# A two-layer decoder on one core: other orders on four engines, the values of the mixture split before the clearings, and another order at the feed-forward's end

## The reference, cut to what matters

```
x = x + L0_attn(layernorm(x))               # 16 query heads of 32, one key and one value head
x = x + L0_xattn(layernorm(x), ctx)         # a mix of features
x = x + L0_ffn(layernorm(x), 4-bit weights) # 1408 hidden: down(silu(gate) * up), then y / rms(y)
x = x + L1_attn(layernorm(x))               # 16 heads, then an out-projection with a bias
x = x + L1_xattn(layernorm(x), ctx, mask)   # 16 query heads of 128, 8 key and value heads, then Wo
x = x + L1_ffn(layernorm(x))                # a mixture: 32 experts of rank 16, the best 2 of each row

def ffn(x):
    gate, up = split(x @ dequant(gate_up).T)
    y = (silu(gate) * up) @ dequant(down).T
    return y / sqrt(mean(y * y) + eps)
```

## Time and profile before

| | us |
|---|---|
| median of 3 runs (2445.82 to 2447.76) | 2447.39 |
| profiled execution | 2444.98 |
| its span | 2443.2 |
| TensorE busy | 2354.3 |
| VectorE busy | 1730.4 |
| ScalarE busy | 1197.0 |
| GpSimd busy | 159.5 |

### The profile page before, as it was taken

One profiled execution on the slowest core, in us unless ns is written; L12 is line 12 of the kernel. 1 busy time (PEld: TensorE's weight loads), 2 busy tenths in 40 slices (PEclk: granted clock), 3 DMA queues, 4 the chain that ended last, 5 costly groups with the idle time before them and its releaser, 6 DMA issues. The chain is left out here.

```text
span 2443.2 us, 37409 instructions
## 1 busy us (share of the span) xinstructions
PE 2354.3 (96%) x11266; PEld 1740.2 (71%) x11266; DVE 1730.4 (71%) x3717; ACT 1197.0 (49%) x2346; POOL 159.5 (7%) x281
## 2 busy tenths in 40 slices
PE   7899999999999899999989999999999999999798
PEld 5555557777777688555557777777777777777677
DVE  6578888877877654667656766667776767667863
ACT  3467766533233522567745544444444444444641
POOL 0000000000000000000031000001010101010200
PEclk9999999999999999999999999999999999999999
DMA  5722201000000235443302000000000000001001
GB/s 169 201 75 72 69 20 69 1 1 0 0 0 1 77 118 181 121 101 93 77 31 74 1 13 12 9 13 9 13 14 8 17 4 17 4 9 45 1 18 52
DMA packets 71922, 110.51 MB, mean 45 GB/s; under 512 B 14266, under 2 KB 25274, under 8 KB 71194
## 3 DMA queue, kind: packets, MB, share of 16 engines
q1 hardware_dynamic: 71834, 109.38, 15.0%
HBM read 75.26 MB, written 34.08 MB: 45 GB/s over the span
## 5 line engine op out<-in xcount | busy, mean ns | idle before, releaser
L3446 DVE SCALAR_TENSOR_TENSOR x_res<-xa_out_bank,xa_den,x_res 128x512 f32 (+1 forms) x256 | 191.6, 748 | 139.2 <-PE xa_out_bank L2921 138.6
L3295 ACT ACTIVATE xa_pT_hi<-xa_t_bank 128x512 fp32r<-128x512 f32 x256 | 149.6, 597 | 128.1 <-PE xa_t_bank L3117 128.1
L333 DVE TENSOR_REDUCE l1s_mx<-l1s_max_bank 128x1 f32<-128x512 f32 x256 | 156.5, 682 | 68.7 <-PE l1s_max_bank L188 68.6
L3306 ACT ACTIVATE xa_prob<-xa_prob,xa_nmax 128x512 f32<-128x512 f32 x256 | 182.7, 715 | 29.6 <-DVE xa_nmax L3413 29.6
L3395 DVE TENSOR_TENSOR xa_pT_lo<-xa_t_bank,xa_pT_hi 128x512 fp32r<-128x512 f32 x256 | 175.7, 687 | 24.1 <-ACT xa_pT_hi L3295 23.8
L333 DVE TENSOR_REDUCE l0s_mx<-l0s_max_bank 128x1 f32<-128x512 f32 x256 | 156.9, 683 | 46.8 <-PE l0s_max_bank L188 46.7
L3413 DVE CUSTOM_DVE_ANT_0 xa_prob<-xa_s_bank,xa_mask_bias 128x512 f32<-128x512 f32 x256 | 171.1, 687 | 22.6 <-PE xa_s_bank L2921 10.9
L3099 PE MATMUL xa_bank_a<-xa_xT_hi,xa_q_w 128*128 (+1 forms) x512 | 180.1, 393 | 0.0
L2921 PE MATMUL xa_out_bank<-xa_o_w,xa_o_hi 128*128 128x512 f32 x512 | 170.2, 413 | 9.5 <-DVE x_res L3446 8.4
L2123 DVE SCALAR_TENSOR_TENSOR ffn_yT<-ffn_y,ffn_ysc,ffn_yT 128x512 f32<-128x512 f32 x164 | 120.6, 746 | 42.5 <-PE ffn_y L1849 42.4
L3117 PE MATMUL xa_t_bank<-ident,xa_prob 128*128 128x128 f32 x1024 | 149.9, 274 | 0.0
(11 more groups left out here) (506 smaller groups left out, 5673.9 us busy)
## 6 DMA issues: line engine op xcount, KB each, us to landing
l0s_q<-l_q SPq DMA_DIRECT2D x96, 128.0 KB, 2.4
l1s_q<-l_q SPq DMA_DIRECT2D x96, 128.0 KB, 3.1
l1s_k<-l_k SPq DMA_DIRECT2D x96, 128.0 KB, 3.2
l0s_k<-l_k SPq DMA_DIRECT2D x96, 64.0 KB, 2.5
x_res<-in_x_dram SPq DMA_DIRECT2D x4, 1024.0 KB, 9.4
l_q<-l_q_hi SPq DMA_DIRECT2D x16, 256.0 KB, 2.5
l_q<-l_q_lo SPq DMA_DIRECT2D x16, 256.0 KB, 3.2
l_q<-l_hi SPq DMA_DIRECT2D x16, 256.0 KB, 2.1
```

The source lines that it names most:

```text
L333: dve.tensor_reduce(self.mx[:, j // QT, j % QT:j % QT + 1], self.max_bank[j % 3][:], AX.X, ALU.max)\
L3295: act.activation(pT_hi[:, kt % (QT - 1), :], t_bank[kt % 2][:], ACT.Copy).then_inc(pT_hi_done, 1)
L3306: act.activation(prob[:, q, :], prob[:, q, :], ACT.Exp, bias=nmax[:, q:q + 1], scale=-1.0, accum_out=den[:, r, 0, q:q + 1]).then_inc(exp_d ...
L3446: dve.scalar_tensor_tensor(xt, out_bank[:], den[:, r, 2, q:q + 1], xt, ALU.mult, ALU.add)\
```

## The change

It has seven parts.

1. Start. The first load of x is cut into two halves with a semaphore each, and VectorE takes the statistics of tiles 0 and 1 behind the first one. The three bias loads get a semaphore of their own, which ScalarE waits for before its first `take`; TensorE waits for the three weight loads alone.
2. Behind layer 1's attention TensorE gets four more matmuls, whose result nobody reads.
3. Feed-forward, TensorE: down product 0 stands behind 10 gate passes, not 8; product 1 behind all 12 and 2 up passes; product 2 behind 7 up passes, not 6.
4. Feed-forward, ScalarE: the nine scalings stand behind `silu(c, 1)`, not ahead of it; in the last chunk `take_h` stands ahead of a `keep`.
5. Feed-forward's end, VectorE: the additions of y stand ahead of the statistics, and the last one ahead of `combine`.
6. Out-projection. GpSimd adds 12 biases, waits for the first scales, adds the last four and waits twice more between the pieces of weights. TensorE projects the first queries ahead of product 15; ScalarE and VectorE take them early. VectorE takes the first maximum ahead of the last `combine`, and it now normalises tiles 12 to 15, which was ScalarE's.
7. Mixture. The tiles are dealt out anew, so that GpSimd splits the values first and then waits for the turned weights and clears `mix_gT_hi`.

```diff
@@ -711,15 +712,18 @@
-            load_x(0)
+            half = S // 2
+            for n, loaded in enumerate((x_loaded[0], x_half_loaded)):
+                sp.dma_start(st.x[:, n * QT // 2:(n + 1) * QT // 2, :],
+                             x_in[0, n * half:(n + 1) * half].rearrange("(q p) d -> p q d", p=P)).then_inc(loaded, 16)
...
             sp.dma_start(bias[:, 0:KC], Wq_b.rearrange("(f p) -> p f", p=P), allow_slow_non_contiguous=True)\
-                .then_inc(w_loaded, 16)
+                .then_inc(bias_loaded, 16)
...
                 sp.dma_start(bias[n * HD:(n + 1) * HD, KC:NF], column(w), allow_slow_non_contiguous=True)\
-                    .then_inc(w_loaded, 16)
+                    .then_inc(bias_loaded, 16)
@@ -804,7 +808,7 @@
             pe.wait_ge(made, 2)
-            pe.wait_ge(w_loaded, 16 * 6)
+            pe.wait_ge(w_loaded, 16 * 3)
@@ -851,6 +855,8 @@
             def take(b, f):
+                if b == 0 and f == 0:
+                    act.wait_ge(bias_loaded, 16 * 3)
@@ -918,7 +924,11 @@
                 dve.wait_ge(x_loaded[b], 16)
-                norm.stats(dve, b, batch_tiles(b))
+                for t in range(b * QT, (b + 1) * QT):
+                    if t == QT // 2:
+                        dve.wait_ge(x_half_loaded, 16)
+                    norm.tile_stats(dve, t)
+                norm.combine(dve, b, batch_tiles(b))
@@ -1642,6 +1652,8 @@
         att.tensor(pe, turn_out_weights)
+        for _ in range(4):
+            pe.matmul(att.max_bank[2][:], self.st.ident_r[:], self.ow[0][:, 0, :], start=True, stop=True)
@@ -1892,21 +1904,22 @@
                         turn_next(0)
-                        gate_up(c, s, b, 0, 4, 8)
+                        gate_up(c, s, b, 0, 4, 10)
...
                         finished(0)
-                        gate_up(c, s, b, 0, 8, 12)
+                        gate_up(c, s, b, 0, 10, 12)
+                        gate_up(c, s, b, 1, 0, 2)
...
                             turn_weights(c + 1, 1)
-                        gate_up(c, s, b, 1, 0, 6)
+                        gate_up(c, s, b, 1, 2, 7)
...
                         finished(2)
-                        gate_up(c, s, b, 1, 6, 12)
+                        gate_up(c, s, b, 1, 7, 12)
@@ -1988,6 +2001,8 @@
                         silu(c, b)
+                        if b == 1 and more and not first:
+                            scale_weights(c + 1)
@@ -1997,10 +2012,9 @@
                             keep(QT * (b - 2) + 1)
+                        take_h(c, b)
+                        if ended:
                             keep(QT * (b - 2) + 2)
-                        take_h(c, b)
-                        if b == 0 and more and not first:
-                            scale_weights(c + 1)
@@ -2225,16 +2239,16 @@
+                last = (NC - 1) % 2
...
                     add_x(t)
-                last = (NC - 1) % 2
+                    add_y(NC - 1, last, B - 1, t - 2)
...
                     front.norm.tile_stats(dve, t)
-                    if t:
-                        add_y(NC - 1, last, B - 1, t - 1)
+                    if t % 2:
+                        add_y(NC - 1, last, B - 1, 2 + t // 2)
                 front.norm.combine(dve, 0, batch_tiles(0))
-                add_y(NC - 1, last, B - 1, 3)
@@ -2322,11 +2336,11 @@
             self.sc.append(sb("mix_sc1", [P, QT, NS], F32))
-        self.spread_r = room[4]
-        self.gT = gT_hi, [room[6], room[8], after_out[0], after_out[1]]
-        self.v_hi, self.v_lo = [room[n] for n in (0, 1, 7, 9)], room[11:15]
+        self.spread_r = room[6]
+        self.gT = gT_hi, [room[4], room[5], after_out[0], after_out[1]]
+        self.v_hi, self.v_lo = [room[n] for n in (0, 1, 8, 9)], room[11:15]
         self.z_hi = room[15:19], z_hi_1
-        self.z_lo = room[19:22] + [room[10]], [room[3], room[5]] + over_attr
+        self.z_lo = room[19:22] + [room[10]], [room[3], room[7]] + over_attr
@@ -2874,8 +2888,13 @@
         k_lo.append(tile("k_lo1"))
-        v_hi, v_lo = ([tile(f"v_{part}{n}") for n in range(2)] for part in ("hi", "lo"))
-        q_hi, q_lo = ([tile(f"q_{part}{n}") for n in range(NR)] for part in ("hi", "lo"))
+        v_hi = [tile(f"v_hi{n}") for n in range(2)]
+        q_hi, q_lo = [tile("q_hi0")], [tile("q_lo0")]
+        v_lo = [tile(f"v_lo{n}") for n in range(2)]
+        for n in range(1, NR):
+            q_hi.append(tile(f"q_hi{n}"))
+        for n in range(1, NR):
+            q_lo.append(tile(f"q_lo{n}"))
@@ -2989,10 +3008,12 @@
-                def split_weights(g):
+                def split_weights(g, after={}):
...
                     for i, (count, n) in enumerate(loaded):
+                        if i in after:
+                            pool.wait_ge(scales_ready, after[i])
@@ -3011,10 +3032,15 @@
-                with pool.Fori(0, T) as t:
-                    xt = st.x[:, bass.ds(t, 1), :].rearrange("p a d -> p (a d)")
-                    pool.tensor_tensor(xt, xt, out_bias[:], ALU.add).then_inc(biased, 1)
-                split_weights(0)
+                def add_bias(t0, t1):
+                    with pool.Fori(t0, t1) as t:
+                        xt = st.x[:, bass.ds(t, 1), :].rearrange("p a d -> p (a d)")
+                        pool.tensor_tensor(xt, xt, out_bias[:], ALU.add).then_inc(biased, 1)
+                add_bias(0, T - QT)
+                pool.wait_ge(scales_ready, 1)
+                add_bias(T - QT, T)
+                split_weights(0, {2: 2, 4: 3})
@@ -3026,8 +3052,6 @@
                 mixture.round_spread(pool)
-                pool.wait_ge(mixture.ring.turned, mixture.U_at[3] + 1)
-                mixture.clear(pool, mixture.gT[0])
@@ -3039,6 +3063,8 @@
                 mixture.rest_values(pool, 3)
+                pool.wait_ge(mixture.ring.turned, mixture.U_at[3] + 1)
+                mixture.clear(pool, mixture.gT[0])
@@ -3240,12 +3266,14 @@
                         project_vT(0)
+                        project_q(0, 0, 0, 12)
...
                 turn_v(0)
-                project_q(0, 0, 0, 12)
+                pe.wait_ge(op_read, T - 1)
                 score(0, 0, 0, 0)
+                pe.wait_ge(op_read, T)
@@ -3370,6 +3398,7 @@
                         take_vT(0)
+                        take_q(0, 0)
@@ -3380,9 +3409,6 @@
                 act.activation(nmax[:, QT:QT + 1], st.ident[:, 0:1], ACT.Exp)
-                take_q(0, 0)
-                for t in range(T - QT, T):
-                    normalise(t)
@@ -3539,9 +3565,12 @@
                         take_k(0, 0)
+                        take_q(0, 0)
...
                     add_projected(t)
+                    if t == T - 1:
+                        maximum(0, 0, 0)
@@ -3549,11 +3578,12 @@
                         bias_of(0)
+                maximum(0, 0, 1)
...
                 scales(B - 1)
-                take_q(0, 0)
-                maximum(0, 0, 0)
-                maximum(0, 0, 1)
+                dve.wait_ge(ring.turned, T - QT)
+                for t in range(T - QT, T):
+                    norm.normalise(dve, t)
```

More of the change, by code:

```diff
@@ L697, in project_and_attend @@
         x_loaded = st.sems(*(f"x_loaded_{b}" for b in range(B)))
-        w_loaded, made, ident_r_made = st.sems("w_loaded", "ident_made", "ident_r_made")
+        w_loaded, bias_loaded, x_half_loaded, made, ident_r_made = st.sems(
+            "w_loaded", "bias_loaded", "x_half_loaded", "ident_made", "ident_r_made")
         projected, kv_ready, klo_done, hi_done, lo_done, v_turned, v_read = st.sems(
```

## The result

| | median us | runs |
|---|---|---|
| before | 2447.57 | 4 (2445.82 to 2447.81) |
| changed | 2428.59 | 4 (2423.12 to 2433.71) |

The ratio is 0.9924, with a 95% interval of 0.9912 to 0.9937: 19 us faster, where 24.6 were forecast. The changed kernel scatters over 10 us in these runs.

What follows compares the result with a forecast made beforehand. TensorE, busy in 96% of the span, was taken as the bound, leaving its gaps and lower-clock stretches to win. Terms 1.3 + 9.8 + 0.3 + 0 + 7.6 + 1.9 + 3.7 = 24.6 us gave a median of 2422.8, range 2413 to 2434.

Steps and rivals of the forecast that it cites:

- the inner one of 2416 to 2428: Whole kernel: the forecast's own narrower range of times in us, given a chance of 0.62.
- Start, 1.3: Kernel start: loading x in halves shortens the chain to the normalised tiles, winning 1.3 us (0.8 to 1.8).
- Feed-forward, 9.8: Feed-forward chunks: the losses at down product 0 in blocks 1 and 2 go, winning 9.8 us (8.3 to 11.1).
- The 1.3 us that I took off for the scalings: Feed-forward, block 2: ScalarE's scalings still leave h_lo late, so 0.15 us stays in each of nine chunks.
- End, 0.3: Feed-forward's end: adding the last y before combine wins 0.3 us (0 to 0.8).
- four matmuls, 0: Behind layer 1's attention: four extra matmuls hidden in a gap, 0 us (a loss of 0.9 to a gain of 1.4).
- Out-projection, 7.6: Out-projection: GpSimd silent beside the first three combines removes waits of 4.93 and 0.73 and 1.9 of lower clock: 7.6 us.
- the price: Out-projection: the last four biases and the weights' pieces come later, hidden by four tiles of work each.
- First queries, 1.9: First scores: q is ready early, ending a 2.55 us wait, partly given back by later maxima: 1.9 us (0 to 3.9).
- Mixture, 3.7: Mixture's third combine: values split earlier remove most of a 2.41 us wait and 1.5 of lower clock: 3.7 us.
- the collision named as a rival: Mixture: GpSimd's value subtractions hold VectorE's small operations in their new place, eating the 3.7: 2426.5 us; chance 0.12.
- the signs that the prediction named: Profile after: feed-forward and op_a_lo waits gone, chunks 1.1 us shorter, L499 at 0.17, clock above 0.95, first projection at 18.1.

Runs made afterwards that it cites:

- e4: The changed kernel run again, unchanged, with a second profile: 2429.11 us (2427.69 to 2430.57).
- e1: The kernel before with the feed-forward's parts 3 and 4 alone (TensorE's order, ScalarE's scalings behind silu): 2440.0 us, ratio 0.9958.
- e5: The changed kernel with TensorE's old order in chunk 0 of the feed-forward: 2427.28 us, ratio 0.9915.
- e2: The kernel before with part 6 alone and the mixture's tiles dealt out as in the changed kernel: 2440.19 us, ratio 0.9971.
- e8: The changed kernel with 14 additional GpSimd clearings of a 128x512 tile beside the first combine: 2428.95 us, one execution.
- e12: The changed kernel with 11 additional GpSimd copies of a 128x512 tile beside the first combine: 2432.38 us, one execution.

## Why the prediction was right, and where it was off

The time lies in the range of 2413 to 2434, 0.6 us above the inner one of 2416 to 2428, and the direction is right. The forecast was 5.8 us too low. By its own steps, the place of each read by laying e4's trace beside that of before:

- **Start, 1.3:** 0.8 on average. The normalised tiles do come 1.3 us earlier. TensorE then waits for Wq, whose load stands behind one more issue, and its transposes run at 0.21 us each until a moment between 13.2 and 17.2 us, and at 0.11 from there. That moment differs from profile to profile.
- **Feed-forward, 9.8:** 11.2 in chunks 1 to 9, all that was there. The 1.3 us that I took off for the scalings did not stay. But the sum counted "the same 9 chunks", those with waits, and left chunk 0 out: it has the same order and is bound by the turned x and by h, not by the matmuls. Two passes ahead of product 0 there put `ffn_u` and all behind it later. It lost 1.7 us in the first profile and 3.2 in e4, where it also ran at the lower clock (as in e1). e5 takes it back.
- **End, 0.3 and four matmuls, 0:** nothing that could be told. The wait for the last y did not go, it is 2.09 us after 1.74. The wait for h ahead of the last products fell from 2.15 to 1.35, which no term had.
- **Out-projection, 7.6:** 8.1. The mechanism, the row and the price were right.
- **First queries, 1.9:** 1.4, and 0.4 where the clock falls behind it (the first profile). The second maximum's wait of 1.20 us takes part of the gain; the prediction had a cost for the maxima, though for the third and fourth.
- **Mixture, 3.7:** 3.6. The third `combine` gave 4.2. Of that 0.6 went to L2699 beside the subtractions: the collision named as a rival is there, with 0.6 us and not 3.7. Another 0.8 went into a stretch at the lower clock at 2285, and 0.7 came back behind the one at 2254, counted below.

These make 25.1, and 21.9 with the 3.2 of chunk 0. To the 15.8 of e4's profile 6.1 are left: 1.6 in the stretch at 2254 us and 2.9 in the one at 2336, 0.5 between chunk 9 and the out-projection, the 0.8 of the start, which this profile does not have, and 0.3 in small ones. So between these two profiles most of it is the lower clock.

This is also the term that was off in the sum for the median. I counted the lower clock as something that belongs to a wait and goes with it, at 1.9 and 1.5 us. At those two places it did go, 1.7 and 1.6 us by the traces, and about 1.1 at the first queries. But it stood elsewhere instead. Against the one profile of before the sum over the kernel grew, from 16.0 us not granted to 21.8 and 26.5. That says more of that profile: its 0.993 is the highest of fourteen (another one has it too, at 2437.25 us, the fastest of e2's eight runs). Over the 42 executions of the kernel before that ran beside the experiments the mean clock is 0.990, or 24 us not granted, and over the nine of the changed kernel 0.991, or 23. So the lower clock stayed about as it was, and what it gave back at three waits must not be counted. An estimate from these figures: 25.1, less the 1.7 that chunk 0 loses at full clock, less 1.7, 1.6 and 1.1, is 19.0, and the medians differ by 19.0. That it comes out so exactly is luck, since each of the terms is good to some tenths.

Of the signs that the prediction named, two did not come. The first projection starts at 19.46 and 19.41 us in the two profiles of the changed kernel, not at 18.1, and a wait for `ffn_h_lo` of 0.98 us stands in chunk 0. The others came. The prediction also took nothing for the clearing, as no row showed small operations beside one. The trace of before has such a place, at 2318.14 (shown under e8).

What is shown: the waits, by the rows; that contention with GpSimd's reading lengthened the `combine`s, by e2, e8 and e12; that the scatter of the changed kernel goes with the clock, by e4 and the four runs. What is not: why the clock fell at 2254 us in one execution and not at the same work in another. TensorE was busy for the same share ahead of both, 1.72 and 1.73 us of 3.4.

On the rule of the Trainium skill, page "SBUF — State Buffer", section "Who interferes with whom": e8 and e12 bear it out for the operations with two inputs: reading held them and clearing did not. The remark in the page's section "Summary: rules for kernel authors" that the second to issue waits until the first has finished fits the additions (1.27 us beside 1.31, ending 0.02 us behind the addition). The TENSOR_SCALARs, with one tensor input, are not under that rule: L502 took 0.53 and 0.90 us beside clearings and 0.47 beside a copy, and in the mixture L2699 took 0.79 beside subtractions. The line on the 2-port modes in "Who interferes with whom", which names `tensor_scalar`, fits all four. That they ran in such a mode is shown by no trace here.

## What to carry to other kernels

A chain that is late in the steady loop is best mended by placing the consumer later and the blocker behind the chain, both together: the later consumer alone gave 4.6 of 11.2 us (the other alone was not run). Look at the first iteration by itself, since another thing may bound it. Work of GpSimd that reads on-chip memory belongs where VectorE has no small operations with two inputs on the path; clearings held a TENSOR_SCALAR alone, by 0.4 us in e8. A sum made from one profile should leave out the lower clock's stretches, or take them from several profiles, because their places change from run to run and their sum hardly did. Where the mean clock of every execution is known, it shows whether the profile is a usual one.

## What the runs showed of the hardware

- A 128x4 operation of VectorE with two inputs (TENSOR_TENSOR) took 0.17 us beside nothing or clearings, 0.46 to 0.56 beside copies of 0.6 us, and 1.27 beside additions of 1.31 us. It was held if it began behind GpSimd's instruction, and ended 0.01 to 0.02 us after it; begun just ahead of it, it took 0.16 or 0.17.
- A 128x4 TENSOR_SCALAR took 0.17 us beside nothing and was held by clearings too: 0.52 to 0.90 us in all of 14 cases over the fourteen profiles.
- TensorE's clock fell behind different waits in executions of the same kernel, for 3.4, 6.8 or 10.2 us in the middle of the program, and the time went with it: 10 us of scatter at mean clocks of 0.989 to 0.992.
- The windows read a clock of 1.00 at the start, while the transposes there take 0.21 us each, twice the 0.11 of the later ones. In all fourteen stored traces the clock's record has its first entry at 13.2 to 17.2 us, where the transposes go over to 0.11, and nothing before it: there the 1.00 is no measurement.
